# Feeding the first expert chunk through TensorE transposes, and splitting the down weights behind each group's work

## The reference

```
scores = softmax(xf @ w_gate)
weights, idx = top_k(scores, 2)
exp_x[e, place] = xf[token]                  # 8 experts x 2048 places x 512
h = einsum('ecd,edf->ecf', exp_x, c_fc)      # 512 -> 1536
a, g = split(h, 2)
h = silu(a) * g                              # 768 wide
exp_out = einsum('ecf,efd->ecd', h, c_proj)  # 768 -> 512
out[token] += weight * exp_out[e, place]
```

## Time and profile before

| | us |
|---|---|
| time of three runs, median (lowest, highest) | 2905.82 (2905.27, 2906.19) |
| the profiled execution, its time | 2904.62 |
| its span, first to last instruction | 2902.8 |
| TensorE busy over the span | 2795.4 (96%) |
| VectorE, ScalarE, GpSimd busy | 1560.2, 1400.3, 1270.3 |
| the expert block's first DMA is issued at | 1289.82 |
| first matmul of the expert block | 1317.88 |

### The profile page before, as it was taken

One profiled execution on the slowest core, in us unless ns is written; L12 is line 12 of the kernel. 1 busy time (PEld: TensorE's weight loads), 2 busy tenths in 40 slices (PEclk: granted clock), 3 DMA queues, 4 the chain that ended last, 5 costly groups with the idle time before them and its releaser, 6 DMA issues.

```text
span 2902.8 us, 53377 instructions
## 1 busy us (share of the span) xinstructions
PE 2795.4 (96%) x17696; PEld 2295.8 (79%) x17696; DVE 1560.2 (54%) x5034; ACT 1400.3 (48%) x3686; POOL 1270.3 (44%) x1917
## 2 busy tenths in 40 slices
PE   6999999999999999938999999999999999999998
PEld 5888888888888888726888888888888888888886
DVE  5788888888888888834333242332332332423331
ACT  5777777777777777723233232232332322323321
POOL 5677777777777777641122222222121212121211
PEclk9999999999999999968999999999999999999999
DMA  4343344444334344335343443434343434343312
GB/s 149 96 112 112 110 118 111 115 112 118 109 100 113 111 112 118 93 95 133 90 91 91 84 99 81 101 81 95 87 95 78 105 77 95 85 86 93 74 30 29
DMA packets 217032, 281.64 MB, mean 97 GB/s; under 512 B 38720, under 2 KB 128832, under 8 KB 215232
## 3 DMA queue, kind: packets, MB, share of 16 engines
q1 hardware_dynamic: 153696, 144.89, 19.2%
q0 software_dynamic: 32768, 67.26, 12.8%
q10 hardware_dynamic: 30304, 66.07, 6.7%
HBM read 109.53 MB, written 67.90 MB: 61 GB/s over the span
## 4 chain that ended last, share of the span: by engine, by line
PE 54%; DMA 1%; SPq 0%; issue 0%; POOL 0%; DVE 0%; ACT 0%; POOLq 0%
PE a_ps L1427 18%; PE g_ps L1427 18%; PE y_ps L1442 18%; DMA out<-y,recs 0%; SPq L1220 0%; DMA xg<-xn_rows,gather_ids 0%; POOL xg L1266 0%; DMA lists<-table 0%; DMA x_quarters<-xg 0%; DVE xe_lo L1361 0%; POOL out L1294 0%; ACT xe_hi L1321 0%; DVE x_turned L1374 0%; ACT y L1354 0%; DVE act_part L1374 0%
## 5 line engine op out<-in xcount | busy, mean ns | idle before, releaser
L1294 POOL DMA_INDIRECT out<-y,recs x128 | 205.7, 1607 | 1186.5 <-ACT y L1354 840.5
L384 POOL TENSOR_SCALAR probs<-probs,row_inv 128x256 f32<-128x256 f32 x1024 | 502.2, 507 | 267.2 <-DVE row_inv L661 261.2
L483 ACT ACTIVATE probs<-probs,low 128x256 f32<-128x256 f32 x1024 | 511.0, 502 | 188.2 <-DVE low L652 165.8
L1401 DVE TENSOR_TENSOR hidden<-act_part,g_ps 128x512 f32<-128x512 f32 x192 | 132.1, 688 | 858.9 <-ACT act_part L1340 858.9
L652 DVE CUSTOM_DVE_ANT_0 probs<-scores_ps,mask_add,row_any 128x256 f32<-128x256 f32 x1024 | 429.0, 474 | 28.8 <-PE scores_ps L969 28.8
L1427 PE MATMUL a_ps<-xe_hi,fc_hi 128*128 128x512 f32 x768 | 300.2, 391 | 39.8 <-DVE xe_lo L1361 39.8
L1427 PE MATMUL a_ps<-xe_lo,fc_hi 128*128 128x512 f32 x768 | 299.8, 390 | 0.0
L1427 PE MATMUL a_ps<-xe_hi,fc_lo 128*128 128x512 f32 x768 | 299.7, 390 | 0.0
L1427 PE MATMUL g_ps<-xe_hi,fc_hi 128*128 128x512 f32 x768 | 299.0, 389 | 0.0
L1427 PE MATMUL g_ps<-xe_lo,fc_hi 128*128 128x512 f32 x768 | 298.8, 389 | 0.0
L1442 PE MATMUL y_ps<-pj_hi,ht_lo 128*128 128x512 f32 x768 | 298.8, 389 | 0.0
(11 more groups left out here) (172 smaller groups left out, 6510.3 us busy)
## 6 DMA issues: line engine op xcount, KB each, us to landing
probs_m<-blocks SPq DMA_DIRECT2D x1024, 64.0 KB
x_quarters<-xg SPq DMA_DIRECT2D x512, 64.0 KB, 2.0
fc_raw<-in_c_fc SPq DMA_DIRECT2D x24, 1024.0 KB, 5.7
out<-x_xn ACTq DMA_DIRECT2D x32, 512.0 KB, 2.8
xn_rows<-x_xn ACTq DMA_DIRECT2D x32, 512.0 KB, 4.9
cin<-in_ctx_t ACTq DMA_DIRECT2D x31, 512.0 KB, 5.8
xin<-in_x ACTq DMA_DIRECT2D x31, 512.0 KB, 4.3
pj_raw<-in_c_proj SPq DMA_DIRECT2D x8, 1536.0 KB, 6.6
```

What stands on the lines that cost most here:

```text
L384: last = nc.gpsimd.tensor_scalar(probs[:, r, t, :], probs[:, r, t, :], row_inv[:, r, t:t + 1], 1.0, ALU.mult, ALU.mult)
L483: last = nc.scalar.activation(probs[:, r, t, :], probs[:, r, t, :], ACT.Exp, scale=-1.0, bias=low[:, r, t:t + 1], accum_out=row_sum[:, r, ...
L1294: nc.gpsimd.indirect_dma_start(out=out[:, :], out_offset=bass.IndirectOffsetOnAxis(ap=recs[:, i * CT + t, 0:1].bitcast(U32), axis=0), in_= ...
L1401: nc.vector.tensor_tensor(hidden[:, m % 2, :], act_part[:, m % 2, :], g_ps[m % 2][:, :], ALU.mult).then_inc(gated, 1)
```

## The change

It has two parts.

The first 512 rows take another way. After the gather, ScalarE copies row tiles t = 0 and 2 and VectorE row tiles t = 1 and 3 inside the partition, from `xg` into `x_quarters` seen in another order (`x_first`), so that the 128 features of each c lie side by side. TensorE turns the 16 squares of 128x128 (c outer, t inner) against an identity matrix into the four banks of the up projection, which hold nothing yet. From the banks ScalarE makes `xe_hi` and VectorE `xe_lo`. The 16 DMAs of chunk 0 and its four block transposes are gone. GpSimd makes the identity in `act_part` before it waits for the lists. SyncE waits for the gather of chunk 0 and then issues the rest of expert 0's weights. The gather of chunk 2 and the 16 DMAs of chunk 1 wait for the last of the 16 transposes. All counts of `quartered` and `x_turned_done` are one chunk lower.

The down weights of a group are split after the group's own `ht_hi` and `ht_lo`, no longer at its head, on both engines and for all eight experts. TensorE no longer waits for all six sixths ahead of the down projection, but in tile t = 0 for sixth m ahead of that m's three matmuls.

```diff
@@ expert_block, tiles
-        def x_turn(later, c):
-
-            return (x_turned[:, :], hidden[:, 0, :], hidden[:, 1, :], act_part[:, 0, :])[0 if later else c]
+        ident = act_part[:, 0, 0:P]
+        x_first = x_quarters.rearrange("p t c (a l) -> p t c a l", l=DK)
+        first_ps = a_ps + g_ps
@@ SyncE
-                    need(sp, x_turned_done, q * DC)
+                    need(sp, x_turned_done, (q - 1) * DC)
+                    if is_step(q, 1):
+                        sp.wait_ge(first_turned, DC)
...
                 load_fc(0, 0)
-                quarter(0)
+                sp.wait_ge(gathered[0], 16 * CT)
+                settle(sp)
                 for j in range(1, PIECES):
                     load_fc(0, j)
@@ GpSimd
+                nc.gpsimd.memset(ident, 0.0).then_inc(ident_ready, 1)
+                pool.wait_ge(ident_ready, 1)
+                nc.gpsimd.affine_select(out=ident, in_=ident, compare_op=ALU.not_equal, fill=1.0,
+                                        base=0, pattern=[[-1, P]], channel_multiplier=1).then_inc(ident_ready, 1)
                 pool.wait_ge(lists_loaded, 16)
...
-                    need(pool, quartered, (q - 1) * QUARTERED)
+                    if is_step(q, 2):
+                        pool.wait_ge(first_turned, DC)
+                    need(pool, quartered, (q - 2) * QUARTERED)
@@ ScalarE
+                def first_order(t):
+                    act.wait_ge(gathered[0], 16 * CT)
+                    nc.scalar.copy(x_first[:, t], xg[:, 0, t, :].rearrange("p (a c l) -> p c a l", c=DC, l=DK)).then_inc(
+                        first_ordered[0], 1)
+
+                def first_turn(c):
+                    act.wait_ge(first_turned, c + 1)
+                    nc.scalar.copy(xt[0][:, 0, c, :], first_ps[c][:, :]).then_inc(xt_hi_done, 1)
 
                 fc_hi(0, 0)
+                for t in range(0, CT, 2):
+                    first_order(t)
                 for c in range(DC):
-                    turn(0, 0, c)
+                    first_turn(c)
                 for m in range(1, MC):
                     fc_hi(0, m)
...
                         for m in range(MC):
-                            if i == 0:
-                                pj_hi(e, m)
...
                             nc.scalar.copy(ht[0][:, m, :], hidden[:, m % 2, :]).then_inc(ht_hi_done, 1)
+                            if i == 0:
+                                pj_hi(e, m)
@@ VectorE
+                def first_order(t):
+                    dve.wait_ge(gathered[0], 16 * CT)
+                    nc.vector.tensor_copy(x_first[:, t], xg[:, 0, t, :].rearrange(
+                        "p (a c l) -> p c a l", c=DC, l=DK)).then_inc(first_ordered[1], 1)
+
+                def first_lo(c):
+                    dve.wait_ge(xt_hi_done, c + 1)
+                    low(xt[1][:, 0, c, :], first_ps[c][:, :], xt[0][:, 0, c, :], xt_split)
 
                 fc_lo(0, 0)
+                for t in range(1, CT, 2):
+                    first_order(t)
                 for c in range(DC):
-                    turn(0, 0, c)
-                    if c:
-                        turn_lo(0, 0, c - 1)
-                turn_lo(0, 0, DC - 1)
+                    first_lo(c)
...
-                            if i == 0:
-                                dve.wait_ge(pj_hi_done, e * MC + m + 1)
-                                low(pj[1][:, m, :], pj_raw[:, m, :], pj[0][:, m, :], pj_split)
...
                             low(ht[1][:, m, :], hidden[:, m % 2, :], ht[0][:, m, :], ht_split)
+                            if i == 0:
+                                dve.wait_ge(pj_hi_done, e * MC + m + 1)
+                                low(pj[1][:, m, :], pj_raw[:, m, :], pj[0][:, m, :], pj_split)
                             if m >= MC - DC and (i < CHUNKS - 1 or not final):
                                 turn_lo(q + 1, (i + 1) % 2, m - (MC - DC))
@@ TensorE
+                pe.wait_ge(ident_ready, 2)
+                for c in range(DC):
+                    for t in range(CT):
+                        pe.wait_ge(first_ordered[t % 2], t // 2 + 1)
+                        last = nc.tensor.transpose(first_ps[c][:, t * P:(t + 1) * P], x_quarters[:, t, c, :], ident)
+                    last.then_inc(first_turned, 1)
...
-                        if i == 0:
-                            pe.wait_ge(pj_split, e * MC + MC)
...
                                 if t == 0:
                                     pe.wait_ge(ht_split, q * MC + m + 1)
+                                    if i == 0:
+                                        pe.wait_ge(pj_split, e * MC + m + 1)
```

More of the change, by code:

```diff
@@ L1178, in expert_block @@
         quartered = sem("quartered")
+        ident_ready = sem("ident_ready")
+        first_ordered = [sem(f"first_ordered{i}") for i in range(2)]
+        first_turned = sem("first_turned")
         x_turned_done = sem("x_turned_done")
@@ L1319, in turn @@
                     need(act, up_done, (q - 1) * MC)
-                    act.wait_ge(x_turned_done, q * DC + c + 1)
-                    nc.scalar.copy(xt[0][:, par, c, :], x_turn(0 if is_step(q, 0) else 1, c)).then_inc(xt_hi_done, 1)
+                    act.wait_ge(x_turned_done, (q - 1) * DC + c + 1)
+                    nc.scalar.copy(xt[0][:, par, c, :], x_turned[:, :]).then_inc(xt_hi_done, 1)
+                def first_order(t):
[5 more added lines that the diff above has]
+                    nc.scalar.copy(xt[0][:, 0, c, :], first_ps[c][:, :]).then_inc(xt_hi_done, 1)
                 fc_hi(0, 0)
+                for t in range(0, CT, 2):
+                    first_order(t)
                 for c in range(DC):
-                    turn(0, 0, c)
+                    first_turn(c)
                 for m in range(1, MC):
@@ L1370, in turn @@
                     if c == 0:
[L1371 to L1374, removed]
+                        dve.wait_ge(quartered, q * QUARTERED)
+                    dve.wait_ge(xt_split, q * DC + c)
+                    nc.vector.transpose(x_turned[:, :].rearrange("p (g l) -> p g l", l=DK),
                                         x_quarters[:, :, :, c * DK:(c + 1) * DK].rearrange(
@@ L1379, in turn_lo @@
                     dve.wait_ge(xt_hi_done, q * DC + c + 1)
-                    low(xt[1][:, par, c, :], x_turn(0 if is_step(q, 0) else 1, c), xt[0][:, par, c, :], xt_split)
+                    low(xt[1][:, par, c, :], x_turned[:, :], xt[0][:, par, c, :], xt_split)
+                def first_order(t):
[5 more added lines that the diff above has]
+                    low(xt[1][:, 0, c, :], first_ps[c][:, :], xt[0][:, 0, c, :], xt_split)
                 fc_lo(0, 0)
+                for t in range(1, CT, 2):
+                    first_order(t)
                 for c in range(DC):
-                    turn(0, 0, c)
-                    if c:
-                        turn_lo(0, 0, c - 1)
-                turn_lo(0, 0, DC - 1)
+                    first_lo(c)
                 for m in range(1, MC):
```

## The result

The changed kernel takes 2895.05 us (median of seven runs, 2893.62 to 2896.70), against 2905.27 us for the kernel before (seven runs, 2902.98 to 2906.53). The ratio is 0.9966, with a 95% interval of 0.9954 to 0.9978: 0.34% faster. The profiled execution has 2895.72 us and a span of 2893.9 us, 8.9 us less than before.

A forecast was written before the change was run, and what follows sets the result against it. TensorE, 96% busy, was taken as the bound, with 28 us without matmuls at the expert block's start. Terms 11.2 + 0.6 - 2.8 = 9.0 us less, 2905.8 - 9.0 = 2896.8 us; 8-in-10 range 2892.5 to 2900.5.

The forecast's parts named there:

- The start: Expert block's first 512 rows: copies and transposes replace 16 DMAs and turns, first up matmul at 1306.7, 11.2 us saved.
- The clock: TensorE's half-clock stretch after the first up matmul: restarted by the pause, lasting 4.55 us, 0.6 us saved.
- The last sixth: Down weights' m = 5 split, ahead of tile 0's last matmuls: a 0.35 us wait in each of eight experts, 2.8 us lost.
- What is late next: Chunk 0 behind the earlier start: weight loads and chunk 1's rows keep enough margin, costed at nothing.
- their lead shrinks by 0.8 us: Expert 0's remaining weight loads: issued 10.4 us earlier, while TensorE starts 11.2 us earlier.
- The other term put at nothing: Chunk 1's 16 DMAs, out by about 1321, VectorE wanting them at 1324.6; costed at nothing even if late.
- A: Last sixth costs no visible wait, or clock up at once, or both: 2894.0 without wait, 2891.8 with clock too; chance 0.18.
- B: Sixths cost 0.6 us per expert, copies at double price, no clock gain: 2900.6 us; chance 0.12.
- C: Wait for down weights' sixth m = 5 far longer, VectorE or ScalarE behind: 2910.8 at 2.1 us per expert; chance 0.03.
- D: Weights or chunk 1's rows arrive too late, TensorE waits in first groups, say 8 of 11 us: 2904.8; chance 0.05.

The follow-up runs named there:

- unblocked: pj_shift with expert 0's last up-weight third and down-weight splits moved behind later groups' work in chunk 0; no time given, TensorE waited 3.2 us ahead of the down tile.
- g2_late: The changed kernel with the gather of chunk 2 held back until expert 0's down weights have landed; ratio 0.9968 to the kernel before.
- pj_shift: The changed kernel with the six down-weight splits behind groups 0, 1, 1, 2, 3, 4; the block's own time 1.6 us shorter than the changed kernel's.
- start_only: The changed kernel with the down-weights part undone, only the first 512 rows' new way kept; 7.1 us of the block's own time gained against the kernel before.
- warm_t: The changed kernel with 60 identity transposes ahead of the 16 real ones; the block's own time 1.3 us longer than the changed kernel's.
- all: unblocked with gathers awaited singly, tile-by-tile transposes, first up group started per feature block, chunk 1's turns behind group work, 56 identity transposes ahead; 2886.65 us.
- pj_only: The kernel before with the down-weights part alone; ratio 1.0005, the block's own time 3.6 us longer.

## Why the prediction was right, point by point

The forecast was 2896.8 us and 9.0 us less; measured are 2895.05 us and 10.2 us less, in the profiled executions 8.9.

Part of that agreement is luck: the clock gave 0.4 us more than forecast and the waits took 0.5 us more, and the two misses cancel.

- **The start.** Forecast for the first up matmul was 1306.7, measured 1306.70. Inside, small errors cancelled: VectorE's copies took 0.76 us and not 1.1, and ScalarE's 1.14 and not 1.24, but they started 0.25 us later. The transposes ended at 1305.29, against 1305.3. The saving of 11.2 us is 11.18, and 11.0 counted from the block's first DMA.
- **The clock.** Forecast was a slow stretch of 4.55 us, measured one of 3.6 (1306.7 to 1310.3), so 1.0 us saved and not 0.6. The assumption that the pause starts the stretch anew is too simple: in unblocked, with the same 16 transposes and the same pause of 1.4 us, the clock was up before the first up matmul. How long the stretch is differs between executions of the same start: 3.6 us in the changed kernel, 3.3 in g2_late, 2.9 in pj_shift, none in unblocked. The forecast has no term for a fall of the clock in mid-stream; start_only and unblocked each had one, behind waits of 3.3 and 3.2 us, and the changed kernel had none. The Trainium skill, "TensorE: Matmul & The Clock Gate", Part 4: PE-mode transpose, says that transposes don't count for the clock; warm_t, all and unblocked disagree, with rises from 1.2 to 2.4 GHz on float32 transposes alone. The measurement decides.
- **The last sixth.** Forecast were eight waits of 0.35 us, 2.8 us; measured are seven of 0.35 and one of 0.8, 3.3 us. The arithmetic from the earlier trace rows held for the seven, and pj_shift showed the cause.
- **What is late next.** This is the step that was sized wrongly. I wrote that the down weights' wait "is eased" and that the gathers beside the loads "may put some us on them, which the margins hold". By "their lead shrinks by 0.8 us" the last third would have landed 5.0 us after the first matmul and the down weights 10.9; they were on hand 7.8 and 14.5 us after it. The two gathers are now beside these loads. In g2_late, without that of chunk 2, the loads were on hand 1.1 and 2.6 us earlier, no more than they scatter between executions; holding back that of chunk 1 was not tried. So the cause of the late landing stays open in part. In the changed kernel this costs 0.5 us, expert 0's longer wait. The margin that I gave as 5 us and more was nearly used up: start_only waited 3.3 us for it and lost 1.7 by the clock, pj_shift waited 1.8, warm_t 2.5. The other term put at nothing, VectorE waiting for chunk 1's rows ahead of the product of group 2, cost nothing in the changed kernel, but in unblocked a wait of 2.4 us there grew into 3.2 us of TensorE and 1.7 of clock.
- **The rivals.** A, no visible waits, is out by pj_only's and the changed kernel's traces, though its clock half can happen. B and C did not occur. D, loads or chunk 1's rows that arrive too late, is the mechanism of four of the experiments, at 1.8 to 5.0 us and not 8.

## What to carry to other kernels

When a stage is started earlier, list every load that the first instructions behind the start stand for, and on which engine what is queued behind them; a load whose issue moves along with the start need not land as much earlier (here the down weights were issued 10.0 us earlier after the block's first DMA, and on hand 6.7 us earlier). Price a wait of TensorE by more than its length: two of 3.2 and 3.3 us here were followed by 3.4 us at half clock, which cost 1.7 us on top. Work on operands that arrive late belongs behind the work that feeds TensorE, but not as the last thing ahead of TensorE's own wait: one subtraction in that place cost 0.35 us each time, and one group earlier it cost nothing in seven experts of eight. Where a difference of 1 to 3 us is in question, time the changed stage from its own first event in the trace, since the stage before it scatters as much.

## What the runs showed of the hardware that was not expected

- Transposes alone raise TensorE's clock from 1.2 to 2.4 GHz, and with pauses of 1.5 and 1.9 us around 16 of them it fell back at 1305.5 (warm_t), while after pauses of less than 0.4 and then 1.2 us it stayed up (all). In the up and down projections it fell for 3.4 us behind waits of 3.3 us (start_only) and 3.2 us (unblocked), and stayed up behind waits of 1.8 us (pj_shift) and 2.5 us (warm_t).
- VectorE's copy of 128x512 floats inside SBUF, reading runs of 32, takes 0.43 us alone (all) and 0.76 us for two (the changed kernel), with GpSimd issuing gathers beside it.
- The load of 1.5 MB of down weights took 15.6 us from issue to landing before and 18.9 us in the changed kernel, behind the same two loads of 1 MB. It scatters: 16.4 us in pj_only, 17.1 to 20.2 us in the seven kernels with the early start and no gather held back, 16.6 us in g2_late.
